# A two-layer attention and feed-forward kernel: the first transposes of P moved ahead of the scores in both halves of a tile

## The reference, cut to what matters

```python
q, k, v = jnp.split(shift_token(x) @ wqkv, 3, axis=-1)      # into 8 heads of 64
q = l2norm(q) * qs
k = l2norm(k) * ksc
q, k = rotary_xpos(q, k)
sim = jnp.einsum('bhwid,bhwjd->bhwij', bq * 8, bk)          # windows of 256 keys, and the 256 before
sim = jnp.where(mask, -max, sim)                            # a band of 256 positions
attn = jax.nn.softmax(sim, axis=-1)
out = jnp.einsum('bhwij,bhwjd->bhwid', attn, bv)
x = x + out @ wo
```

## Time and profile before

| what | value |
|---|---|
| median of 3 runs | 3240.29 us |
| the profiled execution's own time | 3243.91 us |
| its span on the core | 3241.7 us |
| TensorE, matmul busy | 3088.7 us, 95% |
| VectorE busy | 1820.4 us, 56% |
| ScalarE busy | 1490.1 us, 46% |
| GpSimd busy | 1028.4 us, 32% |
| stretch 250 to 960 us (first attention): TensorE busy | 666.18 of 710 us |
| mean granted TensorE clock | 0.98 |

### The profile page before, as it was taken

One profiled execution on the slowest core, in us unless ns is written; L12 is line 12 of the kernel. 1 busy time (PEld: TensorE's weight loads), 2 busy tenths in 40 slices (PEclk: granted clock), 3 DMA queues, 4 the chain that ended last, 5 costly groups with the idle time before them and its releaser, 6 DMA issues.

```text
span 3241.7 us, 48323 instructions
## 1 busy us (share of the span) xinstructions
PE 3088.7 (95%) x16534; PEld 2565.0 (79%) x16534; DVE 1820.4 (56%) x3933; ACT 1490.1 (46%) x3198; POOL 1028.4 (32%) x1670
## 2 busy tenths in 40 slices
PE   9997999999977999999998999999995999999999
PEld 8986888888866788888877888888874788887887
DVE  4655777777765333333324777777775434333332
ACT  2116888888861111111113888888883111111111
POOL 0316555665536000000044565556555100000000
PEclk8999999999988999999999999999997999999999
DMA  4421111111123111101131111111104201111110
GB/s 150 139 77 33 62 61 66 66 66 56 56 59 114 40 40 40 37 3 40 39 119 40 56 66 56 66 66 66 53 27 137 74 14 53 46 52 53 52 39 20
DMA packets 149779, 194.50 MB, mean 60 GB/s; under 512 B 23286, under 2 KB 90998, under 8 KB 149284
## 3 DMA queue, kind: packets, MB, share of 16 engines
q1 hardware_dynamic: 133700, 175.69, 16.3%
q10 hardware_dynamic: 15840, 15.73, 1.5%
HBM read 120.06 MB, written 41.95 MB: 50 GB/s over the span
## 4 chain that ended last, share of the span: by engine, by line
PE 76%; POOL 12%; issue 6%; DVE 3%; ACT 3%; POOLq 0%; DVEq 0%; SPq 0%; ACTq 0%
PE bank L343 21%; PE bank L345 21%; PE bank L344 21%; PE bank L578 4%; PE bank L812 3%; PE bank L774 3%; POOL a_tmp L1634 2%; POOL a_krot L1636 2%; PE bank L791 2%; POOL a_rt L1606 1%; POOL a_rs L1609 1%; DVE a_krot L1314 1%; POOL a_rt L1605 1%; POOL a_rt L1608 1%; ACT a_sq L1011 1%
## 5 line engine op out<-in xcount | busy, mean ns | idle before, releaser
L1171 ACT ACTIVATE f_gate<-bank,f_b 128x512 f32<-128x512 f32 (+1 forms) x176 | 121.2, 689 | 998.8 <-PE bank L345 998.8
L343 PE MATMUL bank<-f_hT_hi,f_w_hi 128*128 128x512 f32 (+1 forms) x1408 | 556.8, 395 | 15.6 <-ACT f_hT_hi L1152 14.3
L1514 DVE SCALAR_TENSOR_TENSOR f_uraw<-bank,f_b,f_gate 128x512 f32<-128x512 f32 (+1 forms) x176 | 132.0, 750 | 752.5 <-ACT f_gate L1171 752.3
L345 PE MATMUL bank<-f_hT_hi,f_w_lo 128*128 128x512 f32 (+1 forms) x1408 | 553.2, 393 | 0.0
L344 PE MATMUL bank<-f_hT_lo,f_w_hi 128*128 128x512 f32 (+1 forms) x1408 | 552.6, 392 | 0.0
L343 PEld LDWEIGHTS bank<-f_hT_hi,f_w_hi 128*128 128x128 f32 (+1 forms) x1408 | 261.1, 185 | 77.8 <-ACT f_hT_hi L1152 15.0
L1066 ACT ACTIVATE a_P<-a_S,a_bias 128x384 f32<-128x384 f32 x512 | 310.1, 611 | 6.6 <-DVE a_bias L1349 6.2
L345 PEld LDWEIGHTS bank<-f_hT_hi,f_w_lo 128*128 128x128 f32 (+1 forms) x1408 | 260.9, 185 | 64.2
L344 PEld LDWEIGHTS bank<-f_hT_lo,f_w_hi 128*128 128x128 f32 (+1 forms) x1408 | 261.1, 185 | 62.6
L1349 DVE CUSTOM_DVE_ANT_0 a_S<-bank,a_masks,a_q 128x384 f32<-128x384 f32 x512 | 295.6, 615 | 26.2 <-PE bank L774 20.7
L1059 ACT ACTIVATE a_P<-a_P,a_inv 128x384 f32<-128x384 f32 x512 | 287.2, 612 | 2.1 <-DVE a_inv L1355 0.5
(11 more groups left out here) (165 smaller groups left out, 6552.2 us busy)
## 6 DMA issues: line engine op xcount, KB each, us to landing
a_h<-x_layer_in SPq DMA_DIRECT2D x128, 128.0 KB, 2.7
a_res<-x_layer_in SPq DMA_DIRECT2D x64, 256.0 KB, 2.8
x_after_attention<-out_tiles SPq DMA_DIRECT2D x64, 256.0 KB, 2.0
f_res<-x_after_attention SPq DMA_DIRECT2D x64, 256.0 KB, 3.2
f_stage<-in_L_ffn_w SPq DMA_DIRECT2D x60, 256.0 KB, 3.4
a_V<-a_V SPq DMA_DIRECT2D x28, 512.0 KB, 5.2
f_h<-x_after_attention ACTq DMA_DIRECT2D x28, 512.0 KB, 4.2
c_x<-in_x SPq DMA_DIRECT2D x32, 256.0 KB, 2.8
```

The lines of the kernel that those rows point to most:

```text
L343: pe.matmul(dst, w[0], m[0], start=start, stop=False)
L345: return pe.matmul(dst, w[1], m[0], start=False, stop=stop)
L1514: dve.scalar_tensor_tensor(f_uraw[0:ROWS[m], m % 2, :], bank[pair_of(u, m, end)][0:ROWS[m], :], f_b1[0:ROWS[m], 0, m:m + 1], f_gate[0:ROWS ...
```

## The change

In both halves of a step one call is moved on TensorE. `p_T(t, 0)` now stands ahead of `scores(t, 1)`, directly behind `pv(t-1, 1)`; and `p_T(t, 2)` now stands ahead of `scores(t+1, 0)`, directly behind `pv(t, 0)`. No instruction is added or removed and no other engine's list changes.

```diff
                         if here(t - 1):
                             pv(t - 1, 1)
                         if here(t):
+                            p_T(t, 0)
                             scores(t, 1)
-                            p_T(t, 0)
                         if here(t + 1):
                             v_project(t + 1)
...
                         if here(t):
                             pv(t, 0)
+                            p_T(t, 2)
                         if here(t + 1):
                             scores(t + 1, 0)
-                        if here(t):
-                            p_T(t, 2)
                         if here(t + 2):
                             k_project(t + 2)
```

## The result

The changed kernel takes 3273.65 us (median of 4 runs, 3272.02 to 3274.90), the kernel before 3240.53 us beside it (4 runs, 3239.17 to 3244.78). The ratio is 1.010, 95% interval 1.0082 to 1.0117: slower by 33 us. The profiled execution took 3272.02 us with a span of 3269.8 us; that of before 3243.91 and 3241.7, so the two traces differ by 28 us and the medians by 33. The kernel after is one line shorter, so its L1318 is L1319 of before, L1313 is L1314, L1010 is L1011. The attention of the second layer lies at about 1750 to 2470 us of the trace, and not at 1890 to 2610 as given above.

What follows compares the result with a forecast made beforehand. The prediction took a loop through the key projection, off-TensorE steps and key transposes as the bound. 22.0 us for 58 tiles plus 0.5 for the ends, on a 3240.3 us median, gave 3262.5 us, range 3250 to 3278.

Steps and rivals of the forecast that it cites:

- What bounds the kernel: A loop of 21.48 us a tile: 10.91 off TensorE with 0.64 slack, 10.6 on TensorE with none.
- First half: p_T(t, 0) ahead of scores(t, 1), between key projection and key transposes: cost 0, covered by the 0.64 us of slack.
- TensorE's key wait: TensorE's wait for VectorE's scaled keys before the key transposes (L578): 0.64 us a tile, forecast to stay at 0.5 to 0.65.
- Second half: p_T(t, 2) ahead of scores(t+1, 0), between key transposes and key projection: waits for a_hT_lo, every loss paid in full.
- the term of 0.38 us a tile: Second half's cost from pv(t, 0) to key projection: 0.27 us wait and 0.11 passages, bounds 0.26 to 0.43.
- Start of the transposes: p_T(t, 2) starts at 716.07 us, 0.06 after VectorE ends a_hT_lo and 0.27 after pv(t, 0) is through.
- Transposes into scores: From p_T(t, 2) to scores(t+1, 0): six transposes take 0.62 us, the change of form adds a gap of 0.09.
- Scores into the projection: From scores(t+1, 0) to the key projection: 0.98 us first to last score row, then 0.31 into the projection.
- The count: The a_hT_lo wait occurs for 29 tiles a layer, 58 in all: 58 x 0.38 = 22.0 us.
- The ends: First and last tiles of each layer: 0 at t = 0, 0.25 us a layer in the last two, 0.5 in all.
- the passages would hide the stall: Rival: cheaper ways between pv, transposes, scores and projection offset the wait, no change, 3240 to 3246 us; chance 0.08.
- the first half pays too: Rival: later masking overruns the slack before the key transposes, 12 to 24 us more, 3275 to 3287 us; chance 0.11.

Runs made afterwards that it cites:

- e5: Kernel before with the six transposes of p_T(t, 1), between key projection and key transposes, issued twice: 3242.74 us against 3244.65 for the kernel before.
- e6: Kernel before with the six transposes of p_T(t, 2), between key transposes and key projection, issued twice: 3283.01 us against 3244.65 for the kernel before.
- e7: Kernel before with the scores of heads 2 and 3 of tile t+1 moved behind k_project(t+2): 3208.18 us against 3244.65 for the kernel before.
- e3: Changed kernel with the wait for a_hT_lo moved to the last three of p_T(t, 2)'s six transposes: 3253.73 us against 3243.95 for the kernel before.
- e4: Kernel before in its old order, with a wait for a_hT_lo added ahead of scores(t+1, 0): 3259.91 us against 3243.95 for the kernel before.
- e9: Kernel before with p_T(t, 2) put between the scores of heads 0 and 1 and those of 2 and 3: 3261.52 us against 3243.23 before.

## Why the prediction was right or wrong

**What bounds the kernel: right.** The loop with a free and a paid stretch fits the turn of every run; e5 and e6 show it directly.

**First half: right in the steady tiles, by a margin larger than I read.** The turn moves by 0.02 us in the first layer and not in the second. The new wait of p_T(t, 1), which I put at 0 to 0.15 us, is there: it starts 0.33 us after the last projection matmul instead of 0.23. TensorE's key wait fell to 0.46 us by the matmuls' row, a little under my 0.5 to 0.65. I took 0.64 for the slack. The weight loads' row of the kernel before says 0.88:

```profile
710.17 0.42 PEld L578 LDWEIGHTS bank<-ident,a_krot 128*128 128x128 f32 x4 [0.88 <-DVE a_krot L1314]
```

and e7, where TensorE does not wait at this place, bears out the larger number:

```profile
718.29 0.82 PE L791 MATMUL bank<-ident,a_P 128*128 128x128 f32 x6
...
719.30 0.48 PE L343 MATMUL bank<-a_wq_hi,a_hT_hi 128*128 128x512 f32 x1
```

From p_T(t, 1) over the key transposes to the next projection it takes 1.01 us there and 710.59 - 708.71 = 1.88 in the kernel before, so the wait costs 0.87. By the turns: e7's should be 21.48 - 0.88 + 0.36 for a visit = 20.96 us with all slack used, and is 20.95. With 0.64 it would be 21.20. The same holds for the new wait. The weight loads' row of the changed kernel

```profile
705.12 0.64 PEld L791 LDWEIGHTS bank<-ident,a_P 128*128 128x128 f32 x6 [0.46 <-issue]
```

says 0.46, the matmuls' row 0.28, and e3 0.44. But where the form changes, a weight loads' row shows time that is no wait. The kernel before, at the transposes behind the scores, where the matmuls' row has no wait, and e4 at its scores:

```profile
717.05 0.64 PEld L791 LDWEIGHTS bank<-ident,a_P 128*128 128x128 f32 x6 [0.26 <-ACT a_P L1059]
```

```profile
701.33 0.19 PEld L774 LDWEIGHTS bank<-a_KT_hi,a_QT_hi 64*128 64x128 f32 x2 [0.39 <-DVE a_hT_lo L1321]
```

In e4 the row says 0.39, the matmuls' row 0.19, and the scores start 0.26 later than before.

**Second half: right in its mechanism, its size too small.** The step that was mis-sized is the term of 0.38 us a tile, which measured 0.57 in the two turns compared (0.54 as a mean over 29 tiles of the first layer, 0.51 in the second). That lies above the 0.43 that I gave as its upper bound, and the turn above my 21.8 to 21.9. By its own steps, against the start of pv:
- Start of the transposes: predicted 1.87 us after, measured 1.96. I took the passage from VectorE to TensorE from the key transposes (0.06); here it is 0.15.
- Transposes into scores: predicted 0.71, measured 0.77. I had the gap from a projection into scores, 0.09; from transposes it is larger.
- Scores into the projection: predicted 1.29, measured 1.25.
- Key projection, and the way from the key transposes to pv: predicted unchanged, measured 0.02 and 0.05 us longer (721.16 to 725.23, 4.07 us, where it was 4.02). With 0.01 on the part off TensorE this closes the sum: 0.09 + 0.06 - 0.04 + 0.02 + 0.05 + 0.01 = 0.19.

**The count: right.** 58 waits, 16.6 us in all by the matmuls' row. Of the 0.57 us, 0.49 lie between pv and the projection: the wait's 0.44 (e3) and some 0.04 for the order (the first half's rows). The other 0.08 are spread over TensorE's rows. As a mean over the steady tiles of the first layer they are 0.04. Of these, 0.03 lie in the query projection, from whose first matmul to the query transposes it is 2.82 us in the kernel before and 2.85 in the changed one. The kernel before has 2.85 there too in its second layer, and a turn of 21.51 instead of 21.48, so the difference arises without the moved transposes as well; its cause is open.

**The ends: not settled.** I had 0.5 us for both layers. In the two traces the 31 turns from a layer's first key transposes to its last take 15.9 us more in the first layer and 13.7 in the second, 29.6 together, where the spans differ by 28 and the medians by 33. From the last key transposes to the last output projection the changed kernel takes 37.64 and 37.62 us, the kernel before 39.64 and 38.41. The mean granted clock of these stretches is 0.82 in both layers of the kernel before (pv at 927.74 us takes 2.41 us there instead of 1.68), and 0.86 and 0.87 in the changed one, so a part of what was gained there may be the clock; no run tests it.

**The rivals.** That the passages would hide the stall was wrong in sign: the order costs a little by itself. That the first half pays too did not come true in the turn. The measured 3273.65 lies in the range but above the likeliest case's own (3256 to 3270). That it still lies inside is in part luck: the range went up to 3278 for the rival of the first half, which did not come true, and not for a dearer second half.

**The sums.** Two were off by little: 3240.3 + 22.5 is 3262.8 and not 3262.5, and the upper bounds, 58 x 0.43 and 2 us for the ends, give 3267 and not 3270.

## What to carry to other kernels

Before moving an instruction, find the loop that sets the period and ask on which side of it the place lies; work and waits cost everything on the one side and, as long as they stay within the slack, nothing on the other, and the busy share tells neither. A wait that a piece of work carries moves with the work: look up when each of its semaphores is raised against when the engine will now arrive. And the same loop shows where to gain: moving 0.5 us of scores across the end of the key projection gave 36 us.

## What the runs showed of the hardware that I had not expected

- Between two pieces of the same form, the slack of TensorE at a wait is nearly what its weight loads show, not its matmuls: 0.88 against 0.64 us at the key transposes, where e7 gives 0.87, and 0.46 against 0.28 at the new wait, where e3 gives 0.44. At a change of form it isn't: e4 gives 0.26 where the rows have 0.39 and 0.19.
- One more visit to the 64-row form, with no matmul added, costs 0.36 us at a granted clock of 1.00, the 2.4 GHz level (e9), 0.17 of it on entering behind transposes.
- After the end of VectorE's instruction TensorE's next one started 0.04 to 0.06 us later at the key transposes and at the scores of e4, but 0.14 to 0.15 us later at the transposes of P behind pv. The cause of the difference is open.
